# Value sums over two score slots at a time: a dense rotary layout through DRAM, and later output steps in the causal attention

## The chip, the cores and the metric

One core of a Trainium2 chip runs the whole program. Its engines are TensorE (PE, matrix products; PEld is its weight load), VectorE (DVE), ScalarE (ACT), GpSimd (POOL) and SyncE (SP, which issues DMAs). The metric is the device time in microseconds (us), median of several runs.

## The reference

Two transformer layers on x of [64, 128, 128] (64 sequences of 128 tokens, width 128), in float32, with a context of 77 rows per sequence. Six parts follow each other, and after each one comes x = layernorm(x + part(x)):

1. an attention by second order Taylor expansion;
2. a cross attention with 16 heads of 64;
3. eight experts (gelu), the best two per token;
4. a causal attention with 16 heads of 8 and ALiBi slopes;
5. a cross attention over the context with 16 heads of 8, RMS norm and rotary positions on q and k;
6. eight experts (swiglu), two per token, and a shared one.

What the change touches is the core of parts 4 and 5:

```python
# 4, causal
scores = einsum('bhqd,bhkd->bhqk', q, k) * scale + alibi_causal
out = einsum('bhqk,bhkd->bhqd', softmax(scores, -1), v)      # 128 x 128 scores per head
# 5, rotary
q, k = apply_rope(rms_norm(q), q_cos, q_sin), apply_rope(rms_norm(k), k_cos, k_sin)
out = einsum('bhts,bhsd->bhtd', softmax(einsum('bhtd,bhsd->bhts', q, k) * D ** -0.5, -1), v)   # 128 x 77 per head
```

## The kernel before

The six parts are six stages, one after another; X stays in SBUF. `softmax_attention` builds three of them by `kind`: "wide" (part 2), "causal" and "rotary". It works on 32 pairs of sequences. A pair has eight slots (k = 0 to 7), each the scores of one sequence for four heads (HU = 4): 4 x 128 columns in the causal kind, 4 x 77 in the rotary. The loop is written out as a software pipeline. Each engine has a function `step(e, roots, f, c, u, mine, ...)` whose arguments are pairs of different age: e and f are being prepared (q, k, values), c has its scores taken, u is one pair older (division, turning back), mine one older still (output product, sum z, layer norm). In a step each engine goes through k = 0 to 7 and does at each k what the code says, in that order; `lagged(c, u, k, lag)` names the slot that was scored lag slots before. Engines meet only by semaphores: an instruction that waits holds everything behind it on its engine.

One slot of scores goes this way. TensorE multiplies qT by the masked keys (L1115 for two causal slots at once, L1129 for a rotary slot) into one of two score banks. Causal: VectorE adds the slopes (`add_slopes`, L1539) into `biased` and takes the row maxima (L1594), GpSimd subtracts them (`take_max`, L749), and ScalarE takes the exponential of all 512 columns (L1258). Rotary: VectorE takes the maxima straight from the bank, and ScalarE takes four exponentials of 77 columns with the maximum as bias (L1289). Then TensorE turns the exponentials, one transpose per head (L1140), TLAG slots after the scores; ScalarE copies them to `probsT` (L1273); and TensorE multiplies them by the values (`late_sum`, L1040), PLAG slots after the scores.

`late_sum` works in strips: the values of a head are a stationary operand of 32 columns (8 values, a 1 for the sum of the exponentials, zeros), and four heads fill the four strips of 32 output rows side by side. An even slot starts the sum in its strip and the odd one after it completes it. After four slots ScalarE copies the sums (L1300, OLAG), TensorE turns them back (`turn_back`, L1027, slots 4 and 6), VectorE divides (`divide`, L1545 and L1549), TensorE turns the outputs (L1055, L1062) and ScalarE copies them; the output product (L1068), z and its statistics (L1524 to L1531), rstd on GpSimd (L798, L800) and the write of X (L1570 on VectorE, L804 on GpSimd in the rotary kind) follow. OT_LAG sets the slots of these: the product at k = OT_LAG, z at 1 + OT_LAG, rstd at 2 + OT_LAG. In the causal kind the residual sum (L793) is at k = 3, the turn of both outputs (`turn_outputs`) at k = 7 of u.

The rotary kind prepares four pairs ahead (LEAD = 4): x turned and q, k multiplied in slots 0 and 1 (`early`), squares, rotation, an inverse root on VectorE (L1360 to L1372), scaling on GpSimd (L811), and `front` in slots 5 (turned q and k) and 7 (values, L852, copied by L888). It also routes tokens for part 6: logits (L997, L1003), choice of two experts on VectorE in pieces, rows sent by GpSimd's indirect DMA (L758). SP loads x (L668) and context (L670) eight pairs ahead, as long as z of eight pairs before is done.

## Time and profile before

| | us |
|---|---|
| median of 3 runs | 2769.44 (2767.96 to 2771.38) |
| the profiled execution, own time | 2773.75 |
| its span, first to last instruction | 2772.0 |

| engine | busy us | share of the span |
|---|---|---|
| PE | 2534.0 | 91% |
| PEld | 1864.5 | 67% |
| DVE | 1904.9 | 69% |
| ACT | 1671.0 | 60% |
| POOL | 1694.9 | 61% |

The causal stage lies between about 1296 and 1828 us of the span, the rotary between 1828 and 2403; the mean granted clock of TensorE over the span is 0.957 of full speed. Shares over the whole span mix six stages with different limits, so the rows further down go by stage and by pair. "Idle before, releaser" behind a row says how long the engine sat idle ahead of it and whose work ended that.

### The profile page before, as it was taken

What the parts mean: (1) busy time and instruction counts of PE and PEld (TensorE: products, weight loads), DVE (VectorE), ACT (ScalarE), POOL (GpSimd) and SP (SyncE); (2) the same over time, 40 slices, a digit from 0 to 9 for tenths busy, and PEclk for the clock granted to TensorE, in tenths of its full rate; (3) what the DMA queues carried; (4) which work ended last, traced back from release to release, by engine and by line L of the source; (5) the groups of instructions that cost most, each with busy time, mean ns of one, the idle gap of its engine ahead of it and who ended that gap; (6) DMA issues with size and microseconds to landing.
All of it is one profiled execution on the core that took longest, in us unless ns stands there. A gap on an engine that the chain in (4) does not pass through costs nothing. (4 is left out here: it accounts for less than half of the span.)

```text
span 2772.0 us, 61590 instructions
## 1 busy us (share of the span) xinstructions
PE 2534.0 (91%) x19168; PEld 1864.5 (67%) x19168; DVE 1904.9 (69%) x5298; ACT 1671.0 (60%) x4543; POOL 1694.9 (61%) x2110
## 2 busy tenths in 40 slices
PE   8998999999999289996999999969999999699996
PEld 6665887877877289993555555547766666458993
DVE  6884677787777355555777777765788886445655
ACT  6773666666665234444766666639888887623334
POOL 3442334555555645554888888846688887724675
PEclk9998999999999699998999999979999999899998
DMA  8932467777774122214100000000011010011336
GB/s 260 338 107 68 151 215 226 234 224 224 223 220 129 54 65 71 72 58 129 58 11 9 9 11 9 7 25 13 16 30 30 30 30 17 30 30 54 93 93 194
DMA packets 274799, 267.86 MB, mean 97 GB/s; under 512 B 30060, under 2 KB 253561, under 8 KB 274096
## 3 DMA queue, kind: packets, MB, share of 16 engines
q1 hardware_dynamic: 256912, 228.42, 27.2%
q0 software_dynamic: 17280, 34.13, 3.6%
q8 instruction: 161, 2.64, 0.4%
q10 hardware_dynamic: 288, 1.38, 0.2%
q14 instruction: 158, 1.29, 0.1%
HBM read 101.24 MB, written 151.85 MB: 91 GB/s over the span
## 5 line engine op out<-in xcount | busy, mean ns | idle before, releaser
L779 POOL TENSOR_TENSOR wide_probs<-wide_exps,wide_inv_sum 128x616 f32<-128x616 f32 x128 | 168.3, 1315 | 305.6 <-DVE wide_inv_sum L1580 293.0
L749 POOL TENSOR_TENSOR causal_exps<-causal_biased,causal_neg_max 128x512 f32<-128x512 f32 x256 | 262.8, 1036 | 76.4 <-DVE causal_neg_max L1594 76.2
L758 POOL DMA_INDIRECT sorted_x<-send,place_i x240 | 244.1, 1017 | 84.2 <-ACT send L1233 44.0
L1289 ACT ACTIVATE rotary_exps<-banks,rotary_neg_max 128x77 f32<-128x77 f32 x1024 | 248.7, 341 | 19.3 <-DVE rotary_neg_max L1594 19.1
L1764 POOL DMA_INDIRECT results<-gelu_tile_out,gelu_dest_i x142 | 140.1, 986 | 142.2 <-DVE gelu_tile_out L1920 120.0
L1539 DVE TENSOR_TENSOR causal_biased<-banks,regions 128x512 f32<-128x512 f32 x256 | 163.6, 680 | 80.7 <-PE banks L1115 80.4
L1764 POOL DMA_INDIRECT results<-swiglu_tile_out,swiglu_dest_i x142 | 144.6, 1019 | 116.7 <-DVE swiglu_tile_out L1915 59.4
L1833 ACT ACTIVATE gelu_hidden<-banks,gelu_slot 128x256 f32<-128x256 f32 x284 | 116.6, 470 | 159.5 <-PE banks L2010 159.4
L1258 ACT ACTIVATE causal_exps<-causal_exps 128x512 f32<-128x512 f32 x256 | 161.2, 630 | 71.4 <-POOL causal_exps L749 71.4
L1594 DVE TENSOR_REDUCE rotary_neg_max<-banks 128x4 f32<-128x308 f32 x256 | 121.7, 475 | 113.5 <-PE banks L1129 105.1
L1273 ACT ACTIVATE causal_probsT<-banks 128x512 f32<-128x512 f32 x256 | 151.6, 592 | 79.3 <-PE banks L1140 79.3
L1140 PEld LDWEIGHTS banks<-first,causal_exps 128*128 128x128 f32 x1024 | 107.2, 141 | 135.6 <-ACT causal_exps L1258 93.1
L1129 PE MATMUL banks<-rotary_keys,rotary_qT 128*128 128x308 f32 x512 | 192.1, 458 | 4.5 <-ACT rotary_exps L1289 4.1
L1091 PE MATMUL banks<-wide_folded,wide_probsT 128*128 128x128 f32 x1280 | 187.7, 278 | 6.8 <-DVE wide_z L1524 3.4
L703 POOL TENSOR_TENSOR rotary_keys<-rotary_kT,rest 128x308 f32<-128x308 f32 x256 | 176.6, 706 | 22.8 <-ACT rotary_kT L894 19.9
L1129 PE MATMUL banks<-wide_keys,wide_xT 128*128 128x308 f32 x512 | 180.7, 434 | 2.4 <-DVE wide_exps L1601 2.2
L1140 PE MATMUL banks<-first,causal_exps 128*128 128x128 f32 x1024 | 167.8, 286 | 12.2 <-ACT causal_exps L1258 12.2
L1273 ACT ACTIVATE rotary_probsT<-banks 77x512 f32<-77x512 f32 x256 | 155.1, 606 | 37.8 <-PE banks L1140 37.2
L1091 PEld LDWEIGHTS banks<-wide_folded,wide_probsT 128*128 128x128 f32 x1280 | 169.1, 194 | 8.1 <-issue 4.5
L1594 DVE TENSOR_REDUCE causal_neg_max<-causal_biased 128x4 f32<-128x512 f32 x256 | 168.0, 677 | 2.7 <-POOL causal_exps L749 2.1
L915 PE MATMUL banks<-regions,wide_v_context 128*128 128x512 f32 (+1 forms) x312 | 163.8, 607 | 5.0 <-ACT wide_staged L1183 3.3
L835 PE MATMUL banks<-wide_ctxT,regions 128*128 128x154 f32 x1024 | 166.5, 296 | 0.7 <-ACT wide_keys L869 0.6
(385 smaller groups left out, 7018.3 us busy)
## 6 DMA issues: line engine op xcount, KB each, us to landing
v_dram<-wide_staged SPq DMA_DIRECT2D x38, 1024.0 KB, 4.4
sorted_x<-blank SPq DMA_DIRECT2D x1, 34848.0 KB, 116.8
sorted_x<-blank SPq DMA_DIRECT2D x24, 1452.0 KB, 8.7
wide_folded<-v_dram SPq DMA_DIRECT2D x128, 256.0 KB
gelu_tile_in<-sorted_x SPq DMA_DIRECT2D x71, 132.0 KB, 2.1
swiglu_tile_in<-sorted_x SPq DMA_DIRECT2D x71, 132.0 KB, 2.1
gelu_back<-results SPq DMA_DIRECT2D x16, 512.0 KB, 8.0
swiglu_back<-results SPq DMA_DIRECT2D x16, 512.0 KB, 5.4
```

The source lines that it names most:

```text
L703: engine.tensor_tensor(keys[:, b, heads], kT[:, pair.c % 2, b, 0:NK].unsqueeze(1).to_broadcast([P, HU, NK]), mask[:, heads].unsqueeze(2).t ...
L749: pool.tensor_tensor(exps[:, (NU * pair.c + m) % ES], biased[:, m % BS].rearrange("p (h n) -> p h n", h=HU), neg_max[:, m % SLOTS].unsquee ...
L758: pool.indirect_dma_start(route["sorted_x"], bass.IndirectOffsetOnAxis(ap=r_place_i[:, b % 2, which, n // 2:n // 2 + 1], axis=0), send[:, ...
L779: pool.tensor_tensor(probs[:, half % SLOTS, 0:HH * NK].rearrange("p (k h) -> p h k", h=HH), exps[:, half % EB], inv_sum[:, half % SLOTS].u ...
L835: last = pe.matmul(f_bank[:, n * 2 * NK:(n + 1) * 2 * NK], product[:, first + n], ctxT[:, s4], start=True, stop=True)
L1091: last = pe.matmul(o_bank[0][:, b * P:(b + 1) * P], probsT[:, half % 2, n * P:(n + 1) * P], folded[:, pair.c % SPARE, b, g, n], start=g == ...
L1129: pe.matmul(s_bank[k % 2][:, 0:HU * NK], q, moving, start=True, stop=True).then_inc(s_ps, 1)
L1140: last = pe.transpose(p_bank[n % 2][0:NK, h * P:(h + 1) * P], exps[:, (NU * pair.c + n) % ES, h], ident)
L1273: act.activation(probsT[0:NK, n % 2], p_bank[n % 2][0:NK], ACT.Copy).then_inc(probsT_done, 1)
L1289: last = act.activation(exps[:, (NU * c.c + k) % ES, h], scores[:, h * NK:(h + 1) * NK], ACT.Exp, bias=neg_max[:, k % SLOTS, h:h + 1])
L1594: dve.tensor_reduce(neg_max[:, k % SLOTS], scores.rearrange("p (h n) -> p h n", h=HU), AX.X, ALU.max, negate=True).then_inc(max_done, 1)
L1764: pool.indirect_dma_start(results, bass.IndirectOffsetOnAxis(ap=dest_i[:, t % YR, j:j + 1], axis=0), tile_out[:, t % YR, j], None, bounds_ ...
```

## The change

In both kinds the products with the values of two slots are made in one block, at the odd slot: eight strip products where there were twice four. In the causal kind (`late_sums`) they come five slots after the scores (PLAG 5, before 4), ahead of the transposes, and `probsT` has four buffers. Its output steps move: division at slots 5 and 6 (before 4 and 6), the turn of the outputs from slot 7 of u to slot 1 of mine, their copy from 0 to 2, OT_LAG from 1 to 3, the X writes to 6 and 7, the residual to 6, the value product to 4. In the last slot of a causal pair (BIAS_AT = 7) GpSimd no longer subtracts the maxima; ScalarE takes four exponentials from `biased` with the maximum as bias. VectorE's waits for free buffers follow this (`scores_taken`).

In the rotary kind the exponentials of two slots lie without gaps (8 x 77 = 616 columns, padded to 640) and are turned in five transposes of 128 columns, two after the even and three after the odd slot. The values have to lie in the same order of rows: they are computed in slot 7 of the early part (four pairs ahead, where the front had them), copied into `v_rows`, stored to DRAM by four DMAs (`store_values`), and loaded by five into `v_dense` (`load_values`), on SP's queue. Two neighbouring strips read the chunk that they share. `dense_sum` makes the eight products. The context has four buffers in place of eight.

```diff
-    FU = {"wide": 7, "causal": 4, "rotary": 2}[kind]
+    FU = {"wide": 7, "causal": 4, "rotary": 1}[kind]
...
-    EARLY = 2
+    EARLY = 3
+    PITCH, HALF_ROWS = 320, 8 * CONTEXT
...
-    OT, OT_LAG = (1, 1) if kind == "causal" else (2, 0)
+    OT, OT_LAG = (1, 3) if kind == "causal" else (2, 0)
...
+            v_rows = sb("v_rows", [P, 8 * PITCH])
+            v_dense = sb("v_dense", [P, 2, 2, 2, CHUNKS, 64])
...
+        exps = sb("exps", {"wide": [P, EB, HH, NK], "causal": [P, ES, HU, NK], "rotary": [P, 2, CHUNKS * P]}[kind])
...
+        probsT = sb("probsT", [P, 4, HU * P] if kind == "causal" else [P, 2, CHUNKS * P])
...
-            return 8 * (j % 2) + 4 * (j // 2) if late else HU * j
+            return 8 * (j % 2) + 4 * (j // 2) if kind == "causal" else HU * j
...
+        BIAS_AT = 7
+
+        def scores_taken(engine, pair, k):
+
+            if k == BIAS_AT:
+                engine.wait_ge(exps_done, pair.count(NU, NU))
+            else:
+                engine.wait_ge(lessened, pair.count(NU - 1, k + 1))
...
+            def store_values(pair):
+                sp.wait_ge(early_done, pair.count(EARLY, EARLY))
+                rows = route["v_dram"][4 * HALF_ROWS * pair.c:4 * HALF_ROWS * (pair.c + 1)].rearrange("(m h k) c -> h k m c", h=4, k=NK)
+                for h in range(4):
+                    sp.dma_start(rows[h], v_rows[0:NK].rearrange("k (m r) -> k m r", r=PITCH)[:, :, 64 * h:64 * h + 64]
+                                 ).then_inc(v_stored, 16)
+
+            def load_values(pair):
+                s = pair.c % 2
+                sp.wait_ge(v_stored, 16 * 4 * (pair.c + 1))
+                if pair.c >= 2:
+                    sp.wait_ge(pv_done, pair.back(2).count(NU, NU))
+                for b in range(2):
+                    for n in range(2):
+                        at = HALF_ROWS * (2 * (2 * pair.c + b) + n)
+                        sp.dma_start(v_dense[:, s, b, n, 0:4], route["v_dram"][at:at + 512].rearrange("(c p) d -> p c d", p=P)).then_inc(v_loaded[s], 16)
+                rows = route["v_dram"][2 * HALF_ROWS * 2 * pair.c:2 * HALF_ROWS * 2 * (pair.c + 1)].rearrange("(m r) d -> r m d", m=4)
+                sp.dma_start(v_dense[0:HALF_ROWS - 512, s, :, :, 4].rearrange("p b n d -> p (b n) d"), rows[512:HALF_ROWS]).then_inc(v_loaded[s], 16)
...
+                if kind == "rotary" and pair is not None:
+                    store_values(pair)
+                if kind == "rotary" and behind[2] is not None:
+                    if behind[2].c == 0:
+                        sp.wait_ge(ready, READY)
+                    load_values(behind[2])
...
-                    if kind == "causal" and lagged(c, u, k, 1) is not None:
+                    if kind == "causal" and lagged(c, u, k, 1) is not None and lagged(c, u, k, 1)[1] != BIAS_AT:
...
-                    if c is not None and kind != "rotary" and k == 3:
+                    if c is not None and kind != "rotary" and k == (6 if kind == "causal" else 3):
...
                 for b in range(2):
-                    last = pe.matmul(f_bank[0:NK, b * P:(b + 1) * P], ctxT[:, s4, b, 0:NK], w["wv"], start=True, stop=True)
+                    last = pe.matmul(f_bank[0:NK, b * P:(b + 1) * P], ctxT[:, f.c % CTX, b, 0:NK], w["wv"], start=True, stop=True)
...
+            if m == 4:
+                if f.c >= 1:
+                    act.wait_ge(v_stored, 16 * 4 * f.c)
+                return act.activation(v_rows[0:NK].rearrange("p (m w) -> p m w", w=PITCH // 4)[:, :, 0:D],
+                                      chip.banks[0:NK, 6, 0:2 * P].rearrange("p (m d) -> p m d", d=D), copy)
...
         FRONT_AT = {"wide": [(0, 0), (1, 0), (2, 0), (3, 0), (4, 0), (5, 0), (7, 0)],
-                    "causal": [(0, 0), (1, 0), (2, 0), (3, 1)], "rotary": [(5, 0), (7, 0)]}[kind]
...
+                    "causal": [(0, 0), (1, 0), (2, 0), (4, 1)], "rotary": [(5, 0)]}[kind]
+        EARLY_AT = [(0, 0), (1, 0), (7, 0)]
+        EARLY_PARTS = (0, 1, 4)
+        LATE = (2,)
+
+        TLAG, PLAG, OLAG = {"wide": (4, 5, 6), "causal": (3, 5, 5), "rotary": (2, 3, 4)}[kind]
+        DIVIDE_AT = (5, 6) if kind == "causal" else (4, 6)
...
+                        if m == 2 and e.c >= LEAD:
+                            pe.wait_ge(turn_done, e.count(TURNS, TURNS))
+                            pe.wait_ge(front_done, e.back(LEAD).count(FU, FU))
+                        if m == 2 and e.c >= LEAD + 2:
+                            pe.wait_ge(norm_done, 2 * (e.c - LEAD - 1))
+                        front_pe(pe, e, EARLY_PARTS[m]).then_inc(early_ps, 1)
...
+            def late_sums(pair, n):
+                b, g = n // UB, n % UB // 2
                 pe.wait_ge(probsT_done, pair.count(NU, n + 1))
-                if n == 0:
+                if n == 1:
                     pe.wait_ge(front_done, pair.count(FU, FU))
-                if j == 0 and pair.back(1).real:
+                if n % UB == 1 and pair.back(1).real:
                     pe.wait_ge(o_done, pair.back(1).count(2, b + 1))
-                for h in range(HU):
-                    strip = 272 * 2 * b + 256 * odd + 32 * (4 * g + h)
-                    last = pe.matmul(o_bank[b][32 * h:32 * h + 32, g * P:(g + 1) * P], values[0:NK, pair.c % 2, strip:strip + 32],
-                                     probsT[0:NK, n % 2, h * P:(h + 1) * P], start=odd == 0, stop=odd == 1)
-                last.then_inc(pv_done, 1)
+                for odd in range(2):
+                    for h in range(HU):
+                        strip = 272 * 2 * b + 256 * odd + 32 * (4 * g + h)
+                        last = pe.matmul(o_bank[b][32 * h:32 * h + 32, g * P:(g + 1) * P], values[:, pair.c % 2, strip:strip + 32],
+                                         probsT[:, (n - 1 + odd) % 4, h * P:(h + 1) * P], start=odd == 0, stop=odd == 1)
+                last.then_inc(pv_done, 2)
+
+            def dense_sum(pair, n):
+                b, g, s = n // UB, n // 2 % 2, pair.c % 2
+                pe.wait_ge(probsT_done, pair.count(NU, n + 1))
+                if n == 1:
+                    pe.wait_ge(v_loaded[s], 16 * 5 * (pair.c // 2 + 1))
+                if n % UB == 1 and pair.back(1).real:
+                    pe.wait_ge(o_done, pair.back(1).count(2, b + 1))
+                for second in range(2):
+                    for strip in range(4):
+                        chunk = strip + second
+                        last = pe.matmul(o_bank[b][32 * strip:32 * strip + 32, g * P:(g + 1) * P],
+                                         v_dense[:, s, b, g, chunk, 32 * (strip % 2):32 * (strip % 2) + 32],
+                                         probsT[:, (NU * pair.c + n) // 2 % 2, chunk * P:(chunk + 1) * P], start=second == 0, stop=second == 1)
+                last.then_inc(pv_done, 2)
...
+                    at = lagged(c, u, k, PLAG)
+                    if kind == "causal" and at is not None and k % 2 == 0:
+                        late_sums(*at)
...
-                        for h in range(HU):
-                            last = pe.transpose(p_bank[n % 2][0:NK, h * P:(h + 1) * P], exps[:, (NU * pair.c + n) % ES, h], ident)
+                        if kind == "rotary":
+                            for m in range(3 if n % 2 else 2):
+                                at = (2 * (n % 2) + m) * P
+                                last = pe.transpose(p_bank[n % 2][:, m * P:(m + 1) * P], exps[:, (NU * pair.c + n) // 2 % 2, at:at + P], ident)
+                        else:
+                            for h in range(HU):
+                                last = pe.transpose(p_bank[n % 2][0:NK, h * P:(h + 1) * P], exps[:, (NU * pair.c + n) % ES, h], ident)
...
-                    if late and u is not None and k in (4, 6):
-                        turn_back(u, (k - 4) // 2)
+                    if late and u is not None and k in DIVIDE_AT:
+                        turn_back(u, DIVIDE_AT.index(k))
...
-                    if at is not None and late:
-                        late_sum(*at)
+                    if at is not None and kind == "rotary" and at[1] % 2 == 1:
+                        dense_sum(*at)
...
-                    if kind == "causal" and u is not None and k == 7:
-                        turn_outputs(u)
+                    if kind == "causal" and mine is not None and k == 1:
+                        turn_outputs(mine)
...
-                    if kind == "causal" and mine is not None and k == 0:
+                    if kind == "causal" and mine is not None and k == 2:
                         keep_outputs(mine)
...
                     if kind == "causal" and lagged(c, u, k, 2) is not None:
                         pair, m = lagged(c, u, k, 2)
-                        act.wait_ge(lessened, pair.count(NU, m + 1))
                         e_slot = exps[:, (NU * pair.c + m) % ES]
-                        act.activation(e_slot, e_slot, ACT.Exp).then_inc(exps_done, 1)
+                        if m == BIAS_AT:
+                            act.wait_ge(max_done, pair.count(NU, m + 1))
+                            if before(pair, m, ES) is not None:
+                                bc, bk = before(pair, m, ES)
+                                act.wait_ge(probsT_ps, bc.count(NU, bk + 1))
+                            for h in range(HU):
+                                last = act.activation(e_slot[:, h], biased[:, m % BS, h * NK:(h + 1) * NK], ACT.Exp,
+                                                      bias=neg_max[:, m % SLOTS, h:h + 1])
+                            last.then_inc(exps_done, 1)
+                        else:
+                            act.wait_ge(lessened, pair.count(NU - 1, m + 1))
+                            act.activation(e_slot, e_slot, ACT.Exp).then_inc(exps_done, 1)
...
+                        if kind == "rotary":
+                            half = (NU * pair.c + n) // 2
+                            if half >= 2:
+                                act.wait_ge(pv_done, 2 * half - 2)
+                            start, columns = 2 * (n % 2) * P, (3 if n % 2 else 2) * P
+                            act.activation(probsT[:, half % 2, start:start + columns], p_bank[n % 2][:, 0:columns], ACT.Copy).then_inc(probsT_done, 1)
+                        else:
+                            if before(pair, n, 4) is not None:
+                                bc, bk = before(pair, n, 4)
+                                act.wait_ge(pv_done, bc.count(NU, bk + 1))
+                            act.activation(probsT[:, n % 4], p_bank[n % 2], ACT.Copy).then_inc(probsT_done, 1)
...
-                        if before(c, k, ES) is not None:
+                        half = (NU * c.c + k) // 2
+                        if kind == "rotary" and half >= 2:
+                            act.wait_ge(probsT_ps, 2 * half - 2)
...
+                            at = (HU * (k % 2) + h) * NK
+                            into = exps[:, half % 2, at:at + NK] if kind == "rotary" else exps[:, (NU * c.c + k) % ES, h]
+                            last = act.activation(into, scores[:, h * NK:(h + 1) * NK], ACT.Exp, bias=neg_max[:, k % SLOTS, h:h + 1])
...
-                    if n is not None and kind != "rotary" and k in ((5, 6) if late else (3, 4)):
-                        s, b = n.c % 4, k - (5 if late else 3)
...
+                            if kind == "causal":
+                                scores_taken(dve, bc, bk)
+                            else:
+                                dve.wait_ge(shifted_done if kind == "wide" else exps_done, bc.count(NU, bk + 1))
```

## Rows read from the trace of the kernel before

**Rows 1.** Stretches of one pair: length, then busy PE, PEld, DVE, ACT, POOL; clock, DMA.

```profile
1602.00:1618.07 16.07, 15.22 (x133) 8.28 (x132) 12.60 (x28) 10.84 (x23) 13.61 (x16) 1.00 0.03 10
...
1906.84:1922.53 15.69, 15.69 (x147) 11.38 (x146) 10.30 (x31) 14.10 (x52) 10.25 (x14) 1.00 0.06 14
...
2155.65:2171.42 15.77, 15.77 (x147) 11.42 (x146) 11.72 (x33) 14.71 (x58) 13.78 (x19) 1.00 0.11 32
...
2171.42:2191.56 20.14, 16.56 (x148) 11.50 (x147) 19.42 (x46) 14.83 (x55) 16.70 (x21) 0.99 0.10 28
```

**Rows 2.** Timeline of TensorE in one causal pair: start, duration, line, operands, idle before.

```profile
1502.19 0.71 PE L842 MATMUL banks<-rest,causal_xT 128*128 128x128 f32 x4
1502.84 1.13 PE L1115 MATMUL banks<-causal_keys,causal_qT 64*128 64x512 f32 x4
...
1505.06 0.66 PE L1140 MATMUL banks<-first,causal_exps 128*128 128x128 f32 x4
1505.64 0.43 PE L1040 MATMUL banks<-causal_probsT,causal_values 128*32 128x128 f32 x8
1506.00 1.13 PE L1115 MATMUL banks<-causal_keys,causal_qT 64*128 64x512 f32 x4
1507.45 0.66 PE L1140 MATMUL banks<-first,causal_exps 128*128 128x128 f32 x4 [0.32 <-ACT causal_exps L1258]
1507.94 0.38 PE L1027 MATMUL banks<-first,causal_sums 128*128 128x128 f32 x2
...
1510.15 0.44 PE L1062 MATMUL banks<-first,causal_o 128*128 128x128 f32 x2 [0.53 <-DVE causal_o L1549]
1510.52 1.13 PE L1115 MATMUL banks<-causal_keys,causal_qT 64*128 64x512 f32 x4
```

**Rows 3.** The same view, one block of eight strips in the Taylor stage.

```profile
102.24 0.65 PE L386 MATMUL banks<-taylor_weights,taylor_v_strip 128*32 128x128 f32 x16
```

**Rows 4.** Groups of instructions by line on ScalarE: total busy, mean ns of one.

```profile
L1289 ACT ACTIVATE rotary_exps<-banks,rotary_neg_max 128x77 f32<-128x77 f32 x1024 | 248.7, 341 | 19.3 <-DVE rotary_neg_max L1594 19.1
...
L1258 ACT ACTIVATE causal_exps<-causal_exps 128x512 f32<-128x512 f32 x256 | 161.2, 630 | 71.4 <-POOL causal_exps L749 71.4
...
L1273 ACT ACTIVATE rotary_probsT<-banks 77x512 f32<-77x512 f32 x256 | 155.1, 606 | 37.8 <-PE banks L1140 37.2
...
L1266 ACT ACTIVATE wide_probsT<-banks 128x384 f32<-128x384 f32 (+1 forms) x256 | 111.1, 434 | 50.8 <-PE banks L1079 34.6
```

**Rows 5.** Timeline, all engines: causal pairs, and the end of the causal stage.

```profile
1507.74 1.27 DVE L1539 TENSOR_TENSOR causal_biased<-banks,regions 128x512 f32<-128x512 f32 x2
...
1514.88 1.13 PE L1115 MATMUL banks<-causal_keys,causal_qT 64*128 64x512 f32 x4
...
1518.13 1.04 POOL L749 TENSOR_TENSOR causal_exps<-causal_biased,causal_neg_max 128x512 f32<-128x512 f32 x1 [1.46 <-DVE causal_neg_max L1594]
...
1825.39 0.20 POOL L798 TENSOR_TENSOR causal_var_eps<-causal_mean_var,causal_eps 128x2 f32<-128x2 f32 x1 [4.92 <-DVE causal_mean_var L1531]
...
1826.40 0.60 DVE L1570 TENSOR_SCALAR X<-causal_z,causal_mean_var,causal_rstd 128x128 f32<-128x128 f32 x2 [1.09 <-POOL causal_rstd L800]
```

**Rows 6.** Timeline of TensorE in one rotary pair.

```profile
2094.08 0.60 PE L1140 MATMUL banks<-first,rotary_exps 128*77 128x128 f32 x4
2094.52 0.38 PE L1027 MATMUL banks<-first,rotary_sums 128*128 128x128 f32 x2
```

**Rows 7.** DMA issues: count, KB each, median us from issue to landing.

```profile
rotary_ctxT<-in_ctxT SPq DMA_DIRECT2D x32, 77.0 KB, 2.2
...
v_dram<-wide_staged SPq DMA_DIRECT2D x38, 1024.0 KB, 4.4
```

**Rows 8.** Three short rotary stretches, columns as in rows 1.

```profile
2078.44:2081.85 3.41, 2.21 (x20) 1.46 (x19) 2.41 (x6) 1.89 (x7) 3.20 (x4) 1.00 0.02 5
2187.66:2191.07 3.41, 1.54 (x19) 1.10 (x18) 3.34 (x6) 2.03 (x8) 3.11 (x4) 1.00 0.06 20
2191.07:2194.49 3.42, 3.42 (x16) 2.98 (x14) 3.00 (x13) 1.67 (x6) 0.92 (x2) 0.50 0.26 66
```

81 lines of the change are left out of this document (41 added, 40 removed).

## The prediction

> **What bounds the kernel now.** Nothing outside two of the six stages is edited, so I read the span stage by stage: the causal attention (1296 to 1828 us) and the rotary attention (1828 to 2403 us), 32 pairs of sequences each. First the rows of busy time per pair [rows 1]. A causal pair lasts 16.07 us, the same for nearly every pair, with TensorE busy 15.22, GpSimd 13.61, VectorE 12.60, ScalarE 10.84. A rotary pair without routing lasts 15.69 us and TensorE is busy for all of it, ScalarE 14.10. With routing it is 15.77 at best (ScalarE 14.71, GpSimd 13.78); about once in four pairs it is 18 to 20 us, and there VectorE is the engine, 19.42 of 20.14. Then the timeline of TensorE inside one causal pair [rows 2]: it waits twice, 0.32 us for an exponential and 0.53 us for the division before the output is turned. So both stages hang on TensorE's list of instructions, with loops through the other engines close behind. A saving on TensorE counts only until one of these loops is longer.
>
> **Sums of two slots in one block.** A block is four strips now and will be eight, and half as many blocks. A block of four holds the next instruction off by 0.36 us (1505.64 to 1506.00), and going into it costs 0.09 us: four transposes take 0.58 us ahead of a block and 0.49 us ahead of something else [rows 2]. The Taylor stage has blocks of eight: 0.65 us from first start to last end against 0.43 us for four, so the second four cost 0.22 us [rows 2, 3]. Two blocks of four cost 2 x (0.36 + 0.09) = 0.90, one of eight 0.36 + 0.22 + 0.09 = 0.67. Saved: 0.23 us per two slots, **0.92 us per pair** in either stage. I could bound it from both sides by 0.09 (only one entry) and 0.45 (the second four free) per block; I take the row of eight, since it has the same 128x32 strips.
>
> **Causal, what TensorE needs.** 15.22 - 0.92 = 14.30 us. The turn of the outputs (0.37 us, 1510.15 to 1510.52) goes from slot 7 to slot 1 of the next pair, so its 0.53 us wait is gone [rows 2]. The value matmuls go from slot 3 to slot 4. GpSimd loses one subtraction in eight (1.0 us). ScalarE does four exponentials of 128 columns with a bias for one of 512. The nearest rows are 0.341 us each for 77 columns and 0.630 for the 512 [rows 4]: at least nothing, at most 4 x 0.5 - 0.63 = +1.4, and I take 4 x 0.34 - 0.63 = +0.7. ScalarE has 5.2 us to spare per pair, so this counts for nothing [rows 1].
>
> **Causal, what is late next.** OT_LAG goes from 1 to 3, which moves the sum z to slot 4, the inverse root (rstd) on GpSimd to slot 5, and the two writes of X on VectorE to slots 6 and 7. So the root is one slot ahead of its reader and no longer two. Take the scores of slot 4 as t = 0. In the trace, with z in front of the biases as it will be, GpSimd starts that slot's subtraction at 3.25 (1514.88 to 1518.13) and takes 1.0, and the piece of keys behind it, of the same 128x512, another 1.0 [rows 5]. Then come variance and root: 1.01 from the start of the one to the start of the X write that waited for it (1825.39 to 1826.40). X write at 6.26; it takes 0.30; then VectorE adds the biases of slots 6 and 7, 1.27, up to 7.83 us [rows 5]. The next pair's first scores wait for that addition (both score banks are in it). TensorE itself would be there at: slots 4 to 7 take 7.68 us now (1502.84 to 1510.52), less the two waits (0.85), two blocks (0.46) and the moved turn (0.37), plus the value matmuls (0.65, 1502.19 to 1502.84): 6.65 [rows 2]. So a **new wait of about 1.2 us** takes the place of the 0.85. Slots 0 to 3 take 8.38 now, less 0.46, less 0.65, plus 0.37: 7.64. Period 7.9 + 7.64 = 15.55, and I take **15.6**: 0.47 us per pair under 16.07, times 31 = **-14 us**. Queued on VectorE behind the X write that waits are the biases of slots 6 and 7, and behind those the whole of TensorE.
>
> **Rotary, TensorE.** The exponentials of two slots now lie dense, 8 x 77 = 616 columns, turned in five transposes of 128 columns where there were eight of 77. Four of 77 take 0.44 us (2094.08 to 2094.52), four of 128 take 0.49 [rows 2, 6]: 8 x 0.11 - 5 x 0.1225 = 0.27 per two slots, 1.07 per pair. The blocks give 0.92 again. In all -2.0 of 15.69. ScalarE copies 256 and 384 columns, mean 0.434 us, and no longer 512, 0.606 us: 8 x 0.17 = -1.4 of 14.10 [rows 1, 4]. So 13.7 for TensorE and 12.7 for ScalarE. But each even slot now has the block and each odd one has none, while scores wait for the exponentials two slots before; the two engines can't both be full, so I take 14.3 without routing (nine pairs, **-1.4 each, -13 us**). With routing GpSimd is busy 13.78 and I give it 14.5 as its least, and the pairs of 18 to 20 us are VectorE's and stay. Over four pairs I take -1.2, 0, -0.8, -1.2, or **0.8 per pair for 23 pairs, -18 us** [rows 1]. Ends: nothing (ScalarE, GpSimd and VectorE hold it) and 2.0 x 32 = -64.
>
> **Rotary, the way through memory.** The values go from v_rows to DRAM in four transfers and come back in five, 616 and 512 or fewer rows of 256 B each. Nothing in the trace has rows this small; the nearest are rows of 308 B, 77 KB, landed after 2.2 us, and the stores of values in the wide stage, 1024 KB, 4.4 us [rows 7]. The store is behind the x load on SP's queue, which waits for z of the pair eight back, in slot 1; five or six issues later it is out (3 us), landed by 5.2 to 7.5 us; ScalarE's copy of the next values waits for it in slot 7, six slots or 11 us later. The load waits for the sums two pairs back (slot 2) and is wanted nine slots on, 17 us. Both are covered by some 4 us or more, so nothing in the steady part; without the cover each microsecond of lateness would stop ScalarE, its exponentials and so TensorE, once a pair. SP has no other urgent load behind it.
>
> The Trainium skill (DMA: Bandwidth & Descriptors, Specifications) speaks against this: under 512 B per row it has the engine read, modify and write. The row of 308 B, 2.2 us for a whole transfer, shows no such price, but it is a load and not a store [rows 7]. If the rule doubled the 4.4 us, the store would land at about 12 us and cost 1 us per pair.
>
> **Rotary, lead-in.** Four pairs are prepared ahead. Each now has value matmuls (twice 0.65 us, as the clock is at half there [rows 2]) and a copy of about 0.4 in the line, and from the second pair on waits for the store of the one before: four issues of 0.6 and 2.2 for landing, 4.6 us [rows 7]. Four times 1.5 to 2, less 1.3 for the matmuls that go from the first real pair, less what VectorE's inverse root was late by anyway, plus 0.6 for larger memsets: **+5 us**, between 1 and 10.
>
> **Sum.** -14 - 13 - 18 + 5 = -40 us, and +4 for a few falls of the clock (below): -36. Against the profiled execution, 2773.75 us (span 2772.0): 2737.8. It lies 4.3 us over the median of the three runs, 2769.44, so the median becomes **2733.4**.
>
> **Rivals.**
> (1) *The clock.* Where TensorE waits for long the clock falls: a stretch with TensorE busy 1.54 of 3.41 us at 1.00 is followed by one at 0.50, that is 1.2 in place of 2.4 GHz [rows 8]. A fall costs half of 3.4, 1.7 us, on slots 0 to 2, which are in the loop. The new wait of 1.2 us in each causal pair could do this where the 0.32 and 0.53 don't. Against it: a stretch with 2.21 busy was not followed by a fall [rows 8], and 3.41 - 1.2 = 2.2. If 24 of 31 pairs fell, +41 us, with the 4 taken back: 2733 + 37 = **2770**; with all 31, +53 - 4, **2782**, slower than before. It decides at 24 pairs. Chance 0.12, of which slower 0.07. The Trainium skill (TensorE: Matmul & The Clock Gate, What's actually happening) has the slow clock as the default that activity lifts, so by it a longer wait is a risk; the trace agrees only in part.
> (2) *Rotary gains nothing.* ScalarE at 14.10 and GpSimd at 13.78 are so near that shorter TensorE lists turn into waits [rows 1]. 2733 + 31 = **2764**. Chance 0.13.
> (3) *The root is in time.* If the X write doesn't hold VectorE, a causal pair is TensorE's 14.3 to 14.7: another 1.0 x 31 = -31, **2702**. Chance 0.15. Against it stands the order of instructions on GpSimd.
> (4) *The store is late.* 1 us per pair or more from 27 pairs: 2733 + 27 = **2760**; from 1.3 us on it eats the whole gain. Chance 0.07.
> The forecast has 0.53. The range leaves out the clock's far end, the store's, and part of (3): **2704 to 2766**. A measurement tells 0.2%, 5.5 us, from no change; so faster is under 2764: 0.53 + 0.15 + half of (2) and (4) and a part of (1), 0.84; same 0.08; slower 0.08.
>
> **What would show it.** Causal: z every 15.6 us; a wait of X writes for rstd; a wait of the first scores for the biases, 1.2 us. If the period is under 15, step "late next" is wrong; if it is over 16 with stretches at 0.50, rival 1 holds. Rotary: blocks of eight at 0.58 to the next start, transposes at 0.1225, pairs of 14.3 at the beginning; no wait of ScalarE for the store outside the lead-in, and the first scores some 5 us later. A steady ScalarE wait in slot 7 would make (4) right.

## The result, and the profile after

The changed kernel takes 2781.74 us (median of 7 runs, 2777.62 to 2789.74), the kernel before in the same comparison 2772.40: ratio 1.0045, 95% interval 1.0033 to 1.0058. It is **slower by 9 us** where 36 us faster was forecast. Its profiled execution has a span of 2779.9 us; the page's busy times of the engines:

```profile
PE 2452.9 (88%) x18784; PEld 1848.6 (66%) x18784; DVE 1934.5 (70%) x5298; ACT 1657.6 (60%) x4639; POOL 1671.2 (60%) x2079
```

TensorE does 81 us less than before (2534.0), and the kernel is slower all the same.

Busy time by stretch of the changed kernel, columns as in [rows 1]: a causal pair, a causal pair with a fall of the clock in it, two short stretches around that fall, and a rotary pair without routing.

```profile
1639.70:1656.10 16.40, 13.77 (x134) 8.67 (x134) 13.50 (x28) 11.46 (x26) 12.69 (x14) 1.00 0.03 10
1621.75:1639.70 17.95, 15.35 (x134) 9.28 (x134) 13.53 (x28) 11.45 (x26) 12.73 (x14) 0.90 0.02 8
1618.60:1622.00 3.40, 1.08 (x10) 0.87 (x10) 2.65 (x4) 1.71 (x3) 2.40 (x3) 0.99 0.00 0
1622.00:1625.40 3.40, 3.40 (x24) 1.48 (x23) 3.37 (x8) 0.63 (x1) 2.04 (x2) 0.51 0.00 0
1938.02:1952.50 14.48, 13.82 (x136) 10.17 (x135) 11.13 (x30) 12.93 (x51) 10.40 (x14) 1.00 0.46 103
```

The causal pair of 16.07 us became one of 16.40, though TensorE is busy 13.8 in it and no longer 15.2. And 13 of the 29 pairs of the steady part last 17.8 to 17.9, since after a stretch with TensorE busy 1.08 of 3.40 us comes one at 0.51. The kernel before had no such stretch there. The rotary pair went from 15.69 to 14.48 [rows 1]. Each stage's first and last z, from the view of one tile (count, min/median/max ns, first and last start):

```profile
L1630 DVE TENSOR_TENSOR causal_z<-banks,causal_residual x32: 412/420/425, 1340.4 to 1854.9; 128x256 f32<-128x256 f32 x32
L1630 DVE TENSOR_TENSOR rotary_z<-banks,rotary_xin x32: 409/412/426, 1924.4 to 2410.7; 128x256 f32<-128x256 f32 x32
```

The same rows of the kernel before:

```profile
L1524 DVE TENSOR_TENSOR causal_z<-banks,causal_residual x32: 424/425/425, 1338.3 to 1824.0; 128x256 f32<-128x256 f32 x32
L1524 DVE TENSOR_TENSOR rotary_z<-banks,rotary_xin x32: 409/424/425, 1891.8 to 2402.7; 128x256 f32<-128x256 f32 x32
```

So the causal stage ends 31 us later, and the rotary z take 486.3 us and no longer 510.9: 25 us given back. The whole loss is the causal stage. Its timeline (all engines; start, duration, line, operands, idle before) shows where:

```profile
1612.85 1.13 PE L1192 MATMUL banks<-causal_keys,causal_qT 64*128 64x512 f32 x4
1613.21 0.41 DVE L1630 TENSOR_TENSOR causal_z<-banks,causal_residual 128x256 f32<-128x256 f32 x1
...
1617.34 1.04 POOL L747 TENSOR_TENSOR causal_keys<-causal_kT,causal_heads 128x512 f32<-128x512 f32 x1
...
1618.61 0.70 POOL L850 TENSOR_TENSOR causal_rstd<-causal_var_eps,causal_power 128x2 f32<-128x2 f32 x1
...
1619.29 1.03 POOL L799 TENSOR_TENSOR causal_exps<-causal_biased,causal_neg_max 128x512 f32<-128x512 f32 x1
1619.35 1.06 DVE L1676 TENSOR_SCALAR X<-causal_z,causal_mean_var,causal_rstd 128x128 f32<-128x128 f32 x1 [2.00 <-POOL causal_rstd L850]
...
1620.33 1.28 DVE L1644 TENSOR_TENSOR causal_biased<-banks,regions 128x512 f32<-128x512 f32 x2
...
1621.75 1.94 PE L1192 MATMUL banks<-causal_keys,causal_qT 64*128 64x512 f32 x4 [2.32 <-DVE causal_biased L1644]
```

Counted from the scores of slot 4 (1612.85), the write of X starts at 6.50 (forecast 6.26), but takes 1.06 us where 0.30 was forecast: it ends 0.09 us after GpSimd's subtraction, which began 0.06 us before it (1619.29 + 1.03). The biases come 0.7 us later for it, and TensorE's first scores of the next pair have waited 2.32 us (2.1 in most pairs). They take 1.94 us, part of it at half the clock, where the row at full clock has 1.13. Over the stage, from the groups by line (busy, mean ns, idle before):

```profile
L1192 PE MATMUL banks<-causal_keys,causal_qT 64*128 64x512 f32 x484 | 147.5, 686 | 61.9 <-DVE causal_biased L1644 61.9
...
L1676 DVE TENSOR_SCALAR X<-causal_z,causal_mean_var,causal_rstd 128x128 f32<-128x128 f32 x60 | 55.6, 927 | 57.2 <-POOL causal_rstd L850 57.2
```

### The profile page after: what moved, and what is told of

The parts are those of the page before. It is cut to its first block and busy times, and to the rows that moved or that the text cites. A ratio compares the mean times of both kernels' runs of the same rounds, so it can differ in the third digit from the quotient of the medians.

```text
span 2779.9 us, 61198 instructions
## 1 busy us (share of the span) xinstructions
PE 2452.9 (88%) x18784; PEld 1848.6 (66%) x18784; DVE 1934.5 (70%) x5298; ACT 1657.6 (60%) x4639; POOL 1671.2 (60%) x2079
## 3 DMA queue, kind: packets, MB, share of 16 engines
q10 hardware_dynamic: 288, 1.38, 0.2%
## 5 line engine op out<-in xcount | busy, mean ns | idle before, releaser
L799 POOL TENSOR_TENSOR causal_exps<-causal_biased,causal_neg_max 128x512 f32<-128x512 f32 x224 | 232.3, 1038 | 132.6 <-DVE causal_neg_max L1703 130.6
L1192 PE MATMUL banks<-causal_keys,causal_qT 64*128 64x512 f32 x512 | 156.3, 687 | 62.4 <-DVE causal_biased L1644 61.9
L1353 ACT ACTIVATE causal_exps<-causal_exps 128x512 f32<-128x512 f32 x224 | 142.9, 638 | 83.0 <-POOL causal_exps L799 82.6
L747 POOL TENSOR_TENSOR rotary_keys<-rotary_kT,rest 128x308 f32<-128x308 f32 x256 | 177.2, 708 | 16.6 <-ACT rotary_kT L948 13.7
L1682 DVE TENSOR_REDUCE wide_exp_sum<-wide_exps 128x8 f32<-128x616 f32 x128 | 101.8, 795 | 83.6 <-ACT wide_exps L1383 83.5
```

Source lines behind the costliest of these rows:

```text
L747: engine.tensor_tensor(keys[:, b, heads], kT[:, pair.c % 2, b, 0:NK].unsqueeze(1).to_broadcast([P, HU, NK]), mask[:, heads].unsqueeze(2).t ...
L799: pool.tensor_tensor(exps[:, (NU * pair.c + m) % ES], biased[:, m % BS].rearrange("p (h n) -> p h n", h=HU), neg_max[:, m % SLOTS].unsquee ...
```

## The experiments

Times are medians; the ratio is to the kernel before on the same chip, with its 95% interval. "Period" is the mean distance of z over the first 29 causal pairs, "falls" how many falls of the granted clock to 0.50 began in them (kernel before: 16.05 and 0).

| kernel | us | ratio | period | falls |
|---|---|---|---|---|
| changed | 2781.74 | 1.0045 (1.0033 to 1.0058) | 17.07 | 13 |
| rotary_alone | 2752.05 | 0.9941 (0.9921 to 0.9960) | 16.05 | 0 |
| causal_alone | 2799.42 | 1.0115 (1.0092 to 1.0138) | 17.05 | 13 |
| subtract_after_write | 2744.13 | 0.9899 (0.9876 to 0.9922) | 15.69 | 0 |
| write_behind | 2717.62 | 0.9812 (0.9796 to 0.9829) | 14.84 | 0 |
| root_first | 2698.33 | 0.9741 (0.9725 to 0.9757) | 14.25 | 0 |
| gpsimd_slot7 | 2782.26 | 1.0035 (1.0019 to 1.0050) | 17.06 | 13 |
| root_first_gpsimd | 2702.54 | 0.9737 (0.9716 to 0.9758) | 14.24 | 0 |
| outputs_early | 2851.13 | 1.0280 (1.0262 to 1.0299) | 19.27 | 25 |
| held_a | 2791.95 | 1.0076 (1.0048 to 1.0105) | 17.24 | 17 |
| held_b | 2842.14 | 1.0255 (1.0237 to 1.0273) | 18.74 | 25 |
| split_blocks | 2724.92 | 0.9830 (0.9809 to 0.9850) | 15.11 | 0 |
| split_rotary | 2706.04 | 0.9767 (0.9748 to 0.9786) | 14.25 | 0 |

### Each stage alone

The function of the kernel before builds one of the two stages (here the causal one, in rotary_alone).

```diff
-        softmax_attention(chip, "causal", n_seq, X, None, {
+        softmax_attention_earlier(chip, "causal", n_seq, X, None, {
```

> The rotary stage as changed, the causal stage as it was before. In the trace of the changed kernel the rotary stage takes 552.5 us (1858.2 to 2410.7) against 575.4 before (1827.4 to 2402.7). If the two parts don't act on one another, this kernel is 23 us faster than before, near 2749 us. If the rotary gain depended on something that the causal stage left behind (clock, queues), it is under 15 or over 30 us.

> The causal stage as changed, the rotary stage as it was before. The causal stage of the changed kernel ended 31 us later than before. Parts that add up give 31 us slower than before, near 2803 us, with the clock of TensorE at 0.50 for 3.4 us about every second pair of the causal stage. If both the loss and the clock falls needed the whole change, the loss is under 20 us.

17 us faster and 30 us slower, where 23 and 31 were expected; together +13.5 against +9.3 for both at once, within what the intervals leave. The parts add up, and they have opposite signs.

### The wait for the root

```diff
+                    if n is not None and kind == "causal" and k == 2 + OT_LAG:
+                        s = n.c % 4
+                        pool.wait_ge(mean_done, n.count(2, 2))
...
                     if kind == "causal" and lagged(c, u, k, 1) is not None and lagged(c, u, k, 1)[1] != BIAS_AT:
                         take_max(*lagged(c, u, k, 1))
```

This is root_first, an edit of the changed kernel: GpSimd's variance and root stand ahead of `take_max` and the keys. In write_behind, also an edit of the changed kernel, VectorE's write stands behind `add_slopes` and the maximum of its slot:

```diff
-                    if n is not None and kind != "rotary" and k in ((6, 7) if late else (3, 4)):
...
+                    if n is not None and kind == "causal" and k in (6, 7):
...
```

> The changed kernel, with variance and root (rstd) of the causal stage ahead of the subtraction and the keys in GpSimd's slot 5; nothing else differs. Theory A, with the wait for rstd as its first half: the write of X waits for rstd no longer and begins 1.5 to 2 us earlier, the first scores wait under 0.7 us, no clock falls are left, period 14.8 to 15.4, 35 to 55 us faster than the changed kernel; the write of X itself still lasts up to 1.0 us, as it still meets a GpSimd instruction. If the length of the write of X (0.9 us where I had 0.3) were the larger half, half of the wait before the first scores stays. Theory B: no more than 20 us.

> The changed kernel, with VectorE's two writes of X in the causal stage put behind the slopes and the maxima of their slot; nothing else differs. Theory A (the write of X at the head of slot 6 waits for rstd and then for GpSimd's subtraction to end, and holds the biases of slots 6 and 7, for which the next pair's first scores wait, and that wait brings the clock down): the wait of 2.0 us per pair before the first scores falls under 0.5, no stretch at 0.50 is left in the causal stage, its period falls from 16.4 and 18.0 us to 14.5 to 15.0, and the kernel is 45 to 60 us faster than the changed one, 2722 to 2737. Theory B (ScalarE's four exponentials of slot 7 hold the maximum of slot 1, and through it GpSimd and ScalarE): the period stays at 16 us or more and no more than 20 us are gained, by the clock alone.

Both take the wait of the scores away, and the clock stays up. With the root first the kernel is 83 us faster than the changed one and 2.6% faster than before: **the best version**. Theory B is out. Its timeline:

```profile
1483.90 0.70 POOL L824 TENSOR_TENSOR causal_rstd<-causal_var_eps,causal_power 128x2 f32<-128x2 f32 x1
...
1485.43 0.34 DVE L1682 TENSOR_SCALAR X<-causal_z,causal_mean_var,causal_rstd 128x128 f32<-128x128 f32 x1
1485.57 1.09 POOL L747 TENSOR_TENSOR causal_keys<-causal_kT,causal_heads 128x512 f32<-128x512 f32 x1
...
1485.84 1.29 DVE L1650 TENSOR_TENSOR causal_biased<-banks,regions 128x512 f32<-128x512 f32 x2
...
1487.56 1.13 PE L1198 MATMUL banks<-causal_keys,causal_qT 64*128 64x512 f32 x4
```

The root is begun 1.5 us before its reader and done 0.8 us before it, the scores don't wait, and a pair of 14.25 us has TensorE busy for 13.9. This write began before GpSimd's instruction and took 0.34; GpSimd's took 1.09 where its like take 1.04. Both kernels beat what was expected, and the order of the two was the other way round: write_behind is 64 us faster than the changed kernel (45 to 60 expected), root_first 83 (35 to 55 expected). With the write behind, the maxima after it come late, and once a pair the transposes wait 0.61 us for an exponential instead.

### How long the write takes

On GpSimd, ahead of `take_max`:

```diff
+                    if kind == "causal" and n is not None and k == 6:
+                        pool.wait_ge(x_written, n.count(2, 1))
```

> The changed kernel, where in slot 6 of a causal pair GpSimd waits for VectorE's first write of X before it subtracts; nothing else differs, and the wait of the write for rstd stays. The forecast took 0.30 us for this write; the changed kernel has about 1.0, each ending as GpSimd's subtraction ends. If that is so because the two engines exclude each other, the write takes 0.3 to 0.4 us now, the wait before the first scores falls from 2.0 to 1.3 us, and the period without a fall of the clock from 16.4 to 15.7 us, the one forecast. Then 22 us faster than the changed kernel (2760) if the clock still falls every other pair, and about 45 (2737) if a wait of 1.3 us leaves it up. If the write is long for another reason, it stays at 1.0 and the kernel is the same or slower by GpSimd's delay.

```profile
1612.24 0.70 POOL L852 TENSOR_TENSOR causal_rstd<-causal_var_eps,causal_power 128x2 f32<-128x2 f32 x1
...
1612.98 0.35 DVE L1678 TENSOR_SCALAR X<-causal_z,causal_mean_var,causal_rstd 128x128 f32<-128x128 f32 x1 [1.95 <-POOL causal_rstd L852]
1613.24 1.28 DVE L1646 TENSOR_TENSOR causal_biased<-banks,regions 128x512 f32<-128x512 f32 x2
1613.40 1.04 POOL L799 TENSOR_TENSOR causal_exps<-causal_biased,causal_neg_max 128x512 f32<-128x512 f32 x1 [0.46 <-DVE X L1678]
...
1614.66 1.13 PE L1194 MATMUL banks<-causal_keys,causal_qT 64*128 64x512 f32 x4 [1.38 <-DVE causal_biased L1646]
```

The write still waits 1.95 us for the root, but takes 0.35; the scores wait 1.38; z comes every 15.67 us, and there is no fall of the clock. **This kernel is the one I had forecast** (wait 1.2, period 15.6; 2733.4 against 2744). An added wait made it 38 us faster. So the 0.7 us of the first write were the two engines excluding each other (the lock). The Trainium skill (SBUF — State Buffer, Who interferes with whom) states it so: a VectorE `tensor_scalar` that can read through both ports and a GpSimd instruction hold the shared pair exclusively, and whichever comes second waits for the whole of the first. The traces agree where the write comes second: 1.06 us for the one begun 0.06 after the subtraction, 0.35 for the one that meets nothing. Each write that took longer than 0.37 us, in this kernel and in all the others, ends 0.08 to 0.09 us after a GpSimd instruction ends.

The order of the recorded starts alone doesn't tell which engine goes first. In root_first 26 writes began 0.14 to 0.18 us before a GpSimd instruction; they took 0.34 and made that one only 0.01 to 0.05 longer. But 15 of its 64 writes began 0.08 to 0.13 us before one and took 1.20 to 1.25, so they were the ones that waited:

```profile
1402.77 1.24 DVE L1682 TENSOR_SCALAR X<-causal_z,causal_mean_var,causal_rstd 128x128 f32<-128x128 f32 x1
1402.89 1.04 POOL L799 TENSOR_TENSOR causal_exps<-causal_biased,causal_neg_max 128x512 f32<-128x512 f32 x1
```

In that kernel these writes don't make TensorE's scores wait.

### The clock, by the wait alone

On root_first, 5 x 480 columns in held_a and 7 x 512 in held_b:

```diff
+                            if k == 6:
+                                dve.tensor_reduce(filler[:, 0:5], biased[:, 1, 0:480].unsqueeze(1).to_broadcast([P, 5, 480]), AX.X, ALU.max)
                             if k % 2 == 0:
                                 add_slopes(c, k)
```

> The kernel with the root first (2698 us, period 14.2, no fall of the clock in the causal stage), and one added instruction: ahead of the biases of slot 6 VectorE takes a maximum over 2400 columns that nobody reads, by the rows of 512 columns in 0.67 us some 2.5 us long. It meets no GpSimd instruction and waits for nothing, but like the late write of X it holds the biases that the next pair's first scores wait for. These had 0.45 us to spare, so the wait is 2.1 us, as in the changed kernel. Theory A (the length of this wait is what brings the clock down): stretches at 0.50 after about every second wait, period 16.3 and 17.8, 13 to 15 falls; the kernel at 2773 to 2790. Theory B (the falls of the changed kernel had to do with what else it did, not with the wait): no falls, period 16.3, 2698 + 29 x 2.1 = 2759.

> The same with 3584 columns, some 3.8 us, so a wait of 3.3 us. Theory A: a fall after every wait, period 17.5 + 1.5 = 19.0, kernel near 2698 + 29 x 4.8 = 2837; if the falls don't get denser with a longer wait, 2810 to 2820. Theory B: no falls, 2698 + 29 x 3.3 = 2794.

A row of the scores and the two short stretches around its start in held_a, then one of held_b:

```profile
1610.59 1.82 PE L1199 MATMUL banks<-causal_keys,causal_qT 64*128 64x512 f32 x4 [1.96 <-DVE causal_biased L1651]
```

```profile
1607.20:1610.60 3.40, 1.44 (x20) 1.12 (x12) 3.40 (x4) 1.77 (x4) 2.08 (x3) 1.00 0.00 0
1610.60:1614.00 3.40, 3.40 (x23) 1.53 (x24) 3.37 (x8) 0.63 (x1) 2.04 (x2) 0.54 0.00 0
```

```profile
1602.48 2.08 PE L1199 MATMUL banks<-causal_keys,causal_qT 64*128 64x512 f32 x4 [3.19 <-DVE causal_biased L1651]
```

The added instruction meets no GpSimd instruction, as expected, but the write of X ahead of it does once in some seven pairs: it takes 1.20, and the wait of the scores is then 3.04 to 3.07 us in held_a and 4.27 in held_b.

```profile
1381.88 1.20 DVE L1683 TENSOR_SCALAR X<-causal_z,causal_mean_var,causal_rstd 128x128 f32<-128x128 f32 x1
1381.96 1.04 POOL L748 TENSOR_TENSOR causal_keys<-causal_kT,causal_heads 128x512 f32<-128x512 f32 x1
...
1386.98 1.13 PE L1199 MATMUL banks<-causal_keys,causal_qT 64*128 64x512 f32 x4 [3.04 <-DVE causal_biased L1651]
```

In held_a 15 of the 25 waits of 1.96 us have a fall of the clock with them (beginning in it or up to 1.5 us after it) and 2 of the 4 longer ones, in held_b 21 of the 25 waits of 3.2 us and all 4 longer ones. So a wait that was put in by hand brings the falls back, and theory A holds; but not every such wait has one, and the two of 3.04 without a fall show that its length alone doesn't decide. (2791.95 us is just above the 2773 to 2790 expected for held_a, 2842.14 above the 2837 for held_b.) In held_b a pair without a fall is 17.52 us and one with a fall 18.5, 19.0 or 20.1. The last have the longer wait, 1.07 of the 2.5 us; so a fall costs 1.0 to 1.5. The wait of 1.38 above had none, nor had the two of 1.60 and 1.74 us in that kernel. For the changed kernel the price is: its 13 pairs with a fall are 19.1 us over 16.40, 1.47 us each.

### ScalarE in the last slot

```diff
-        BIAS_AT = 7
+        BIAS_AT = None
...
-                engine.wait_ge(lessened, pair.count(NU - 1, k + 1))
+                engine.wait_ge(lessened, pair.count(NU, k + 1))
```

> The changed kernel, where GpSimd subtracts the maxima in the last slot of a causal pair too and ScalarE takes one exponential of 512 columns there, as before the change. Theory A (root and write of X hold the pair; ScalarE's part counts for nothing, as forecast): the time is the changed kernel's within 6 us, 2776 to 2788. Theory B (the wait of the maximum of slot 1 for ScalarE's four exponentials, 1.0 to 2.3 us in each pair of the changed kernel, is on the path): 20 us faster or more. Theory C (GpSimd's relief was worth something even so): 10 us slower or more.

> Variance and root ahead of the subtraction and the keys in GpSimd's slot 5, and GpSimd subtracts in the last slot of a causal pair too, as before the change. Beside the kernel that only has the root first (2698 us, period 14.2, all of it TensorE's), this one shows what ScalarE's part is worth where nothing else holds the pair. If nothing: 2694 to 2704. If GpSimd, then busy about 13.7 of 14.2 us, becomes late: 0.3 to 0.8 us per pair, 2708 to 2724.

Nothing in either surrounding: 2782.26 against 2781.74, and 2702.54 against 2698.33 with overlapping intervals. The maximum's wait for ScalarE's four exponentials (43.0 us over the stage) is real in the trace and off the path.

### The output steps where they were

```diff
-    OT, OT_LAG = (1, 3) if kind == "causal" else (2, 0)
+    OT, OT_LAG = (1, 1) if kind == "causal" else (2, 0)
...
-                    if kind == "causal" and mine is not None and k == 1:
-                        turn_outputs(mine)
+                    if kind == "causal" and u is not None and k == 7:
+                        turn_outputs(u)
...
```

> The changed kernel, where the causal output steps lie as before the change: outputs turned in slot 7 of u, product in slot 1, z in 2, root in 3, writes of X in slots 5 and 6, residual in 3; the blocks of eight and ScalarE's slot 7 stay. Theory A: the root is two slots ahead of its reader again, so no write of X waits for it; TensorE needs 14.3 us per pair and waits some 0.5 us for the division before it turns the outputs; period 14.6 to 15.2, no falls of the clock, 2720 to 2740. If the later output steps were needed for the blocks (the division comes one slot later now), the wait before the turn grows over 1 us and the kernel is above 2745.

A clear miss, 69 us slower than the changed kernel. VectorE and TensorE, around the turn of the outputs:

```profile
1616.88 1.06 DVE L1676 TENSOR_SCALAR X<-causal_z,causal_mean_var,causal_rstd 128x128 f32<-128x128 f32 x1 [1.21 <-POOL causal_rstd L850]
...
1619.05 0.88 DVE L1676 TENSOR_SCALAR X<-causal_z,causal_mean_var,causal_rstd 128x128 f32<-128x128 f32 x1
1619.86 1.27 DVE L1644 TENSOR_TENSOR causal_biased<-banks,regions 128x512 f32<-128x512 f32 x2
...
1621.92 0.29 DVE L1655 TENSOR_TENSOR causal_o<-banks,causal_inv_total 128x128 f32<-128x128 f32 x1
...
1622.27 0.44 PE L1139 MATMUL banks<-first,causal_o 128*128 128x128 f32 x2 [2.04 <-DVE causal_o L1655]
```

The writes of X (1.06 and 0.88, and 1.21 of waiting) now lie ahead of the division, and TensorE waits 2.04 us for that in slot 7, with 25 falls in 29 pairs. So the blocks of eight do need the later output steps, or at least shorter writes; what of the 69 us each of these would give back wasn't tried, nor was this order with the root first.

### The price of a block

On root_first, the strips of the even slot ahead of the transposes and those of the odd one behind them (split_blocks; split_rotary does it with `dense_sum`, the first four ahead of the transposes):

```diff
-                        late_sums(*at)
+                        late_sums(*at, 0)
...
+                    if kind == "causal" and at is not None and k % 2 == 0:
+                        late_sums(*at, 1)
```

> The kernel with the root first, and in the causal stage the block of eight strip products split in two of four with the transposes of the slot between them; the same products, buffers and output steps. In this kernel TensorE has no wait over 0.3 us in a causal pair, so the cost of a block shows in full. By the term of the forecast (a block of four 0.36 and its entry 0.09 twice, against 0.67): 4 x 0.23 = 0.9 us per pair, 29 pairs, 2698 + 27 = 2725. If only the entry counts, 4 x 0.09, 2708; if the second four were free, 4 x 0.45, 2750.

> The kernel with the root first, and in the rotary stage the block of eight split in two of four, one ahead of the transposes of the slot and one where it was. Pairs without routing last 14.3 us with TensorE busy 13.5 of them, those with routing 15.2 to 18.5. By the term of the forecast 0.9 us more of TensorE's work per pair: if TensorE holds the stage, 9 pairs by 0.9 and 22 by some 0.5, 15 to 20 us slower, 2713 to 2718. If it is held by the chain through ScalarE, less than 5 us, 2698 to 2703.

```profile
1602.73 0.42 PE L1107 MATMUL banks<-causal_probsT,causal_values 128*32 128x128 f32 x8
1603.08 0.66 PE L1230 MATMUL banks<-first,causal_exps 128*128 128x128 f32 x4
1603.67 0.43 PE L1107 MATMUL banks<-causal_probsT,causal_values 128*32 128x128 f32 x8
1604.02 0.44 PE L1095 MATMUL banks<-first,causal_sums 128*128 128x128 f32 x2
```

A causal pair of split_blocks lasts 15.14 us, that is 0.89 over root_first, for the term of 4 x 0.23 = 0.92, and 2725 where 2725 was expected. In the rotary stage the same work costs only 0.3 us per pair without routing (73.1 for the first five against 71.6) and 0.1 with; 8 us in all, between the two theories. The forecast's two limits together would give this: TensorE needs 13.7 and another chain holds 14.3, so 0.9 more makes 14.6 (measured 14.76). Which chain that is, without routing and with it, no run separates.

## Why the forecast was wrong

**What bounds, and blocks of eight: right.** 0.92 us per causal pair, measured as 0.9. In root_first, where no other chain holds the pair, it is 14.25 us; the forecast's need was 14.30. That this agrees so well is in part luck: TensorE is busy 13.9 us of the 14.25 (15.22 before), 0.4 less than the 0.92 saved would leave, and the rest of the pair is short waits, 0.2 for a copy by ScalarE and 0.12 at a turning back. Where the other 0.4 of busy time went stays open.

**ScalarE's slot 7 "for nothing": right**, and so was its size: four exponentials take 1.28 us for 0.63, +0.65 against the +0.7 taken.

**Causal, what is late next: the chain right, one term wrong.** Named were the write of X waiting for the root, behind it the biases of slots 6 and 7, behind these TensorE. All of it is in the trace, at 6.50 for 6.26, and slots 0 to 3 of the next pair take 7.70 us (1605.15 to 1612.85) for the 7.64 worked out. The step that failed is "it takes 0.30". It was read at the end of the stage [rows 5], where GpSimd has no work left. In the new place the write is released by a GpSimd instruction, and GpSimd's next instruction, of 1.04 us, starts in the same moment and wins. The trace of before held the sign, a spread of three to one in one form of instruction:

```profile
L1570 DVE TENSOR_SCALAR X<-causal_z,causal_mean_var,causal_rstd x64: 340/379/1060, 1345.6 to 1826.7; 128x128 f32<-128x128 f32 x64
```

Of these 64 all but four are longer than 0.37 us, and each of the 60 ends 0.08 to 0.09 us after a GpSimd instruction.

The price: 16.40 against 15.67 with the write at 0.35, **0.7 us x 29 = 21 us**.

**The clock, rival 1: the mechanism right, the chance of 0.12 far too low.** The wait became 2.1 us and not 1.2, and what spoke against the rival (a stretch in which TensorE idled 1.2 us was not followed by a fall [rows 8]) spoke for a wait of 1.2 alone. At 1.38 there is in fact no fall. 13 falls of 1.47 us, **19 us**; the forecast had 1.7 each. So the sign was settled by two effects in a row: the lock, 21 us, brought the wait to where the clock, 19 us, came in. Rival 1 was priced from 24 falls on as slower; with the lock it took 13.

**The sum.** 0.09 (15.69 for 15.6), 0.72 (the lock; 16.41 is the mean of the 16 pairs without a fall) and 0.66 (the clock) are 1.47 us per pair, 29 pairs, 43 us, of the 45 between -36 forecast and +9 measured. The rest are differences of 1 to 4 us: the first causal z is 2.2 us later, 29 pairs and not 31 are steady, the 4 for falls elsewhere were not all spent, and 3 in the rotary stage.

**Rival 3, "the root is in time": 2702** was its time, and root_first, which makes it so by order alone, has 2698. The chain that I had held against it was "the order of instructions on GpSimd"; that order was free to change.

**Rotary: right.** Without routing the first five intervals of z have a mean of 14.30 (14.3 forecast; TensorE busy 13.8, ScalarE 12.9, for 13.7 and 12.7). With routing 22 intervals are shorter by 0.80 each, -17.6 for -18. What holds the 0.5 us between TensorE's work and the pair wasn't separated by a run. The error in size is in the nine pairs without: the last four gained 0.6 together and the first five 6.3, -7 for -13. The lead-in made up for it: from the last causal z to the first rotary one 69.5 us against 67.8, +1.7 for +5. Rival 2 is out.

**The way through memory: right.** Waits of ScalarE for the store, over the rotary stage (us, times, longest), and one of them:

```profile
ACT rotary_v_rows L941 <- DMA v_rows<-rotary_v_rows: 5.8, 3, 2.0
```

```profile
1875.62 0.38 ACT L941 ACTIVATE rotary_v_rows<-banks 77x256 f32<-77x256 f32 x1 [1.87 <-DMA v_rows<-rotary_v_rows]
```

Three times, all in the lead-in. There the copy before ended at 1870.49, so the store took 5.1 us from there, issues and landing (4.6 forecast). Rival 4 is out. The Trainium skill (DMA: Bandwidth & Descriptors, Specifications) has rows under 512 B read, modified and written; the doubling that the forecast weighed for this isn't in the 5.1 us, with rows of 256 B.

## What to carry to other kernels

When a step is moved to just behind a GpSimd instruction, take its duration not from a place where GpSimd is idle but from its longest one, and ask what GpSimd starts next: this fp32 `tensor_scalar` from SBUF to SBUF on VectorE lasted until that was over. Where an engine waits for a two-column result of another, put that result first in the other's slot; here this order alone is worth 83 us. A forecast whose new wait on TensorE is near a length at which the clock has been seen to fall should carry the fall in its middle case, since any term sized too small leads straight into it.

## What the runs showed of the hardware

- The write of X (128x128, fp32) takes 0.33 to 0.35 us alone. When it took longer than 0.37, in any of the kernels, it ended 0.08 to 0.09 us after a GpSimd instruction: 1.06 when it began 0.06 into GpSimd's subtraction of 1.04 us, 0.79 when it began 0.33 into it, and 1.20 to 1.25 when it began 0.08 to 0.13 ahead of a GpSimd instruction. Begun 0.14 to 0.18 ahead, it took 0.34. Making GpSimd wait 0.46 us for it made the whole kernel 38 us faster.
- Once per pair of 15.7 to 18.7 us, a wait of TensorE of 1.36 to 1.74 us was never followed by a granted clock of 0.50 (29 waits). One of 1.96 was in 15 of 25, one of 2.1 in 13 of 29, one of 3.0 to 3.1 in 2 of 4, one of 3.2 in 21 of 25, one of 4.27 in 4 of 4. A fall of 3.4 us cost 1.0 to 1.5 us, the two of 6.8 us in held_a some 2.3. Why the wait of 1.96 brought more falls than that of 2.1 stays open; the pairs of the two kernels differ in length.
- Eight strip products of 128x32 in a row hold the next instruction off for 0.57 us, and two blocks of four with work between them cost 0.22 us more than one of eight (0.89 for the four of a pair).
